# An LSTM with a three-layer sign-weight network: where x's later quarters are split into high and low parts

## What is computed

```python
def lstm_forward(x, h0, Wx, Wh, b):          # x (32, 64, 256), Wx and Wh (256, 1024)
    xW = einsum('ntd,dg->ntg', x, Wx) + b
    def step(carry, xw_t):
        prev_h, prev_c = carry
        a = xw_t + prev_h @ Wh
        i, f, o = sigmoid(a[:, :256]), sigmoid(a[:, 256:512]), sigmoid(a[:, 512:768])
        g = tanh(a[:, 768:])
        next_c = f * prev_c + i * g
        next_h = o * tanh(next_c)
        return (next_h, next_c), next_h
    ...                                       # 64 steps, one after the other

def ffn(x, k0, k1, k2, s0, s1, s2):           # boolean k: weights are +1 or -1
    h = concatenate([x, -x], axis=-1)
    h = relu(s0 * dense(k0, h)) * 2           # 512 -> 1024
    h = relu(s1 * dense(k1, h)) * 2           # 1024 -> 1024
    return s2 * dense(k2, h)                  # 1024 -> 256

return x + ffn(lstm_forward(x, cond_1024, Wx, Wh, b), ...)
```

## Time and profile before

| what | value |
|---|---|
| three runs | 293.06, 294.0, 294.33 us, median 294.0 |
| the profiled execution | 293.16 us, of which the span 291.4 |
| mean granted clock of TensorE | 0.988 of full speed |
| busy: TensorE matmuls | 277.7 us, 95% of the span |
| busy: VectorE, ScalarE, GpSimd | 206.2, 153.1, 12.0 us |

### The profile page before, as it was taken

One profiled execution on the slowest core, in us unless ns is written; L12 is line 12 of the kernel. 1 busy time (PEld: TensorE's weight loads), 2 busy tenths in 40 slices (PEclk: granted clock), 3 DMA queues, 4 the chain that ended last, 5 costly groups with the idle time before them and its releaser, 6 DMA issues.

```text
span 291.4 us, 8783 instructions
## 1 busy us (share of the span) xinstructions
PE 277.7 (95%) x3608; PEld 224.1 (77%) x3608; DVE 206.2 (71%) x749; ACT 153.1 (53%) x470; POOL 12.0 (4%) x19
## 2 busy tenths in 40 slices
PE   7947997999999999999999999999999999999995
PEld 5835876776799898999989999999999996544441
DVE  2842888877878888888888888888888876531013
ACT  4662564576666655655656556565566544411110
POOL 0108031000000000000000000000000000000000
PEclk9995999999999999999999999999999999999999
DMA  7950000000000000100000001000100100010001
GB/s 191 403 240 2 1 3 2 0 2 2 1 2 2 2 4 2 38 2 3 9 31 3 2 3 38 2 2 3 38 1 2 38 3 2 0 36 2 0 0 72
DMA packets 4791, 8.72 MB, mean 30 GB/s; under 512 B 912, under 2 KB 2448, under 8 KB 4624
## 3 DMA queue, kind: packets, MB, share of 16 engines
q1 hardware_dynamic: 4176, 7.87, 7.6%
q10 hardware_dynamic: 576, 0.30, 0.3%
HBM read 6.07 MB, written 2.10 MB: 28 GB/s over the span
## 4 chain that ended last, share of the span: by engine, by line
PE 74%; DVE 10%; ACT 5%; issue 4%; DMA 3%; SPq 2%; POOL 1%; POOLq 0%; DVEq 0%
PE WK L390 45%; PE ACC L403 9%; PE G L355 9%; PE G L346 8%; PE WK L373 4%; DMA x<-in_x 3%; ACT tT L530 3%; DVE aT L679 2%; DVE cD L690 1%; DVE uT L688 1%; ACT tC L535 1%; DVE xw L586 1%; DVE h L571 1%; POOL xs L727 1%; DVE h L696 1%
## 5 line engine op out<-in xcount | busy, mean ns | idle before, releaser
L390 PE MATMUL WK<-h,k 128*128 128x256 f16 (+1 forms) x992 | 126.9, 276 | 0.1
L390 PEld LDWEIGHTS WK<-h,k 128*128 128x128 fp8e5 x992 | 93.6, 98 | 16.0 <-issue 1.9
L530 ACT ACTIVATE tT<-aT 128x128 f32<-128x128 f32 x126 | 39.0, 310 | 64.2 <-DVE aT L679 62.9
L571 DVE SCALAR_TENSOR_TENSOR h<-WK,h 128x256 f16<-128x256 f32 (+1 forms) x104 | 42.3, 437 | 27.2 <-ACT h L493 27.2
L679 DVE TENSOR_REDUCE aT<-G 128x128 f32<-128x256 f32 x128 | 48.2, 417 | 15.5 <-PE G L355 14.8
L493 ACT ACTIVATE h<-WK 128x256 f16<-128x256 f32 (+1 forms) x104 | 37.2, 388 | 30.0 <-PE WK L390 29.8
L373 PE MATMUL WK<-xs,wxs 128*128 128x512 f32 x168 | 45.7, 412 | 6.2 <-POOL xs L727 5.7
L475 ACT ACTIVATE G<-xw 128x256 f32<-128x256 f32 x126 | 46.6, 370 | 0.0
L373 PEld LDWEIGHTS WK<-xs,wxs 128*128 128x128 f32 x168 | 30.7, 193 | 13.0 <-POOL xs L727 7.0
L346 PEld LDWEIGHTS G<-h,w 128*128 128x128 f16 x1008 | 32.7, 96 | 8.9 <-DVE h L696 6.2
L355 PE MATMUL G<-h,w 128*128 128x64 f16 x1008 | 39.5, 192 | 0.0
(11 more groups left out here) (63 smaller groups left out, 142.2 us busy)
## 6 DMA issues: line engine op xcount, KB each, us to landing
x<-in_x SPq DMA_DIRECT2D x3, 512.0 KB, 8.9
out_y<-x SPq DMA_DIRECT2D x12, 128.0 KB, 1.8
xw<-in_wx SPq DMA_DIRECT2D x4, 256.0 KB, 6.2
xw<-in_wh SPq DMA_DIRECT2D x4, 256.0 KB, 6.5
k<-in_k SPq DMA_DIRECT2D x1, 1024.0 KB, 11.0
k<-in_k SPq DMA_DIRECT2D x1, 512.0 KB, 8.2
out_y<-x SPq DMA_DIRECT2D x2, 256.0 KB, 2.0
x<-in_x ACTq DMA_DIRECT2D x1, 256.0 KB, 4.3
```

Of the source, the lines that this page charges most:

```text
L390: ins = eng.matmul(layer_src(tile), w, rhs, start=a == 0, stop=last)
L530: eng.activation(tT[:, B * j0:B * j1], aT[:, j0:j1].rearrange("p j b -> p (j b)"), ACT.Tanh, scale=half_gain0 if t == 0 else half_gain).th ...
L571: eng.scalar_tensor_tensor(layer_dst(tile, 1), layer_src(tile), 0.0, layer_dst(tile, 0), ALU.max, ALU.subtract).then_inc(lo_made[tile[0]])
```

## The change

1. GpSimd keeps only the two casts of quarter 1 (semaphore `xh1`). Its six subtractions and the other four casts go.
2. The low parts of quarter 1 are made by VectorE ahead of step 0, between `w_lo` and the low part of h0. Quarters 2 and 3 are split by ScalarE (`x_hi`) and VectorE (`x_lo`), one half after each of the steps 2, 3 (quarter 2) and 4, 5 (quarter 3). On ScalarE the split stands ahead of the step's tiles.
3. Tiles of quarters 1 to 3 are all emptied by ScalarE; VectorE empties only tile (0, 4). The six matmuls of such a tile now use the low part of x last.
4. `w0_make` comes after the steps 1, 6, 7; `w2_make` after 6; `w1_make` is two operations on 1024 words, after 8 and 9, of the kind with one tensor input and two operands of one value for each partition (`seven`, `sign1`).
5. Ahead of step 0, `w_max(3)` comes ahead of `wx_lo(2)`, and `wx_lo(3)` comes behind the scales; on ScalarE tile (0, 3) is emptied between the halves of `w_hi`.
6. The order of quarter 3's tiles and of the first layer's first chunk is shifted by a place.

```diff
-X_DVE = ((4,), (2, 5), (2, 5), (2, 5))
+X_DVE = ((4,), (), (), ())
-W0_STEPS = (1, 3, 4)
-W1_STEPS = (5, 6, 7, 9)
-W2_STEPS = (11,)
+X2_STEPS = (2, 3)
+X3_STEPS = (4, 5)
+W0_STEPS = (1, 6, 7)
+W1_STEPS = (8, 9)
+W2_STEPS = (6,)
...
-        order += [((0, 0, m), 4), (("x", 3, m), 6)]
+        order += [(("x", 3, n), 6) for n in range(NJ) if (0, 1, 2, 4, 5, 6, 7, 8)[n] == m] + [((0, 0, m), 4)]
+    order.append((("x", 3, 7), 6))
...
+                if i:
+                    k, wp, xp = ((0, 0, 0), (0, 1, 0), (1, 0, 0), (1, 1, 0), (0, 0, 1), (1, 0, 1))[a]
...
-            def x_hi(k):
-                e.wait_ge(dx0[k], 16)
-                eng.activation(xs[:, 0, 0, k, :], x[:, 0, k], ACT.Copy).then_inc(xh)
+            def x_hi(i, k):
+                if i == 0:
+                    e.wait_ge(dx0[k], 16)
+                else:
+                    e.wait_ge(dx[i - 1], 16)
+                    e.wait_ge(x_mm, NJ * (i - 1))
+                eng.activation(xs[:, i % 2, 0, k, :], x[:, i, k], ACT.Copy).then_inc(xh)
...
+                if t in X2_STEPS:
+                    x_hi(2, X2_STEPS.index(t))
+                if t in X3_STEPS:
+                    x_hi(3, X3_STEPS.index(t))
                 for tile in act_plan[t]:
...
             def w1_make(n):
-                part = k1[:, 512 * n:512 * n + 512]
+                part = k1[:, 1024 * n:1024 * n + 1024]
                 e.wait_ge(dk1, 16)
-                eng.scalar_tensor_tensor(part, part, 7, sign1[:, :].broadcast_to((P, 512)), ALU.logical_shift_left,
-                                         ALU.bitwise_xor).then_inc(w1_made)
+                eng.tensor_scalar(part, part, seven[:, :], sign1[:, :], ALU.logical_shift_left,
+                                  ALU.bitwise_xor).then_inc(w1_made)
...
             w_max(2)
-            wx_lo(2)
             w_max(3)
...
-            wx_lo(3)
+            wx_lo(2)
             e.wait_ge(max_all, 1)
...
+            wx_lo(3)
             x_empty(("x", 0, 4))
             for g in range(4):
                 w_lo(g)
+            x_lo(1, 0)
+            x_lo(1, 1)
...
-            for i in range(1, NQ):
...
-                for k in range(2):
...
-                    eng.tensor_tensor(lo, x[:, i, k], hi.bitcast(F32), ALU.subtract).then_inc(xp_lo)
+            eng.wait_ge(dx[0], 16)
+            for k in range(2):
+                eng.tensor_copy(xs[:, 1, 0, k, :], x[:, 1, k]).then_inc(xh1)
```

More of the change, by code:

```diff
@@ L118, in ready @@
         if tile[0] == "x":
-            inputs = t >= (-1, -1, 2, 6)[tile[1]]
+            inputs = t >= (-1, -1, 4, 6)[tile[1]]
         elif tile[0] == 0:
@@ L211, in lstm_ffn @@
         sign1 = sb("sign1", [P, 1], U32)
+        seven = sb("seven", [P, 1], U32)
         h1 = sb("h1", [P, 8192], F16)
@@ L366, in x_matmul @@
                     e.wait_ge(wxh, j // 2 + 1)
[L367 to L370, removed]
+                if xp:
+                    e.wait_ge(xl, 2 * i + k + 1)
+                elif i == 1:
+                    e.wait_ge(xh1, k + 1)
                 else:
-                    e.wait_ge(xp_lo if xp else xp_hi, 2 * (i - 1) + k + 1)
+                    e.wait_ge(xh, 2 * max(i - 1, 0) + k + 1)
                 ins = eng.matmul(TILE[bank[tile]][:, :], wxs[:, wp, j, k], xs[:, i % 2, xp, k], start=a == 0, stop=a == 5)
@@ L386, in layer_matmul @@
                     e.wait_ge(lo_made[0], 8 * c + k + 1)
-                    e.wait_ge(w1_made, 4)
+                    e.wait_ge(w1_made, 2)
                     w, rhs = w1[:, k, 128 * m:128 * m + 128], h1s[c][:, k, part]
@@ L472, in seed @@
                     wait_x_out(e, ("x", t // 16, 3 if t == 0 and g == 0 else 7))
-                    wait_x_out(e, ("x", t // 16, X_DVE[t // 16][-1]))
+                    if t == 0 and g == 1:
+                        wait_x_out(e, ("x", 0, 4))
                 src = xw[:, t // 4, 4 * g:4 * g + 4].rearrange("p j (t b) -> p j t b", t=4)[:, :, t % 4]
@@ L501, in _ @@
             wx_hi(0)
-            x_hi(0)
-            x_hi(1)
+            x_hi(0, 0)
+            x_hi(0, 1)
             wx_hi(1)
@@ L509, in _ @@
             wx_hi(3)
+            w_hi(0)
+            w_hi(1)
             x_empty(("x", 0, 3))
-            for g in range(4):
-                w_hi(g)
+            w_hi(2)
+            w_hi(3)
             e.wait_ge(scaled, 4)
@@ L563, in w_lo, with x_lo @@
                 eng.scalar_tensor_tensor(lo, src, scale2 if g == 0 else scale, hi, ALU.mult, ALU.subtract).then_inc(wlo)
-            def x_lo(k):
-                e.wait_ge(xh, k + 1)
-                eng.tensor_tensor(xs[:, 0, 1, k, :], x[:, 0, k], xs[:, 0, 0, k, :].bitcast(F32), ALU.subtract).then_inc(xl)
+            def x_lo(i, k):
+                if i == 1:
+                    e.wait_ge(xh1, k + 1)
+                else:
+                    e.wait_ge(xh, 2 * max(i - 1, 0) + k + 1)
+                eng.tensor_tensor(xs[:, i % 2, 1, k, :], x[:, i, k], xs[:, i % 2, 0, k, :].bitcast(F32),
+                                  ALU.subtract).then_inc(xl)
             def layer_lo(tile):
@@ L613, in signs @@
                 e.wait_ge(signed, 6)
+                e.wait_ge(zeroed, 3)
             def w0_make(n):
@@ L621, in w0_make @@
                 elif n == 1:
-                    eng.scalar_tensor_tensor(b, b, 7, sign0[:, :].broadcast_to((P, 512)), ALU.logical_shift_left,
-                                             ALU.bitwise_xor).then_inc(w0_made)
+                    eng.tensor_scalar(b, b, seven[:, :], sign0[:, :], ALU.logical_shift_left,
+                                      ALU.bitwise_xor).then_inc(w0_made)
                 else:
@@ L639, in _ @@
             wx_lo(0)
-            x_lo(0)
-            x_lo(1)
+            x_lo(0, 0)
+            x_lo(0, 1)
             e.wait_ge(db, 16)
@@ L701, in _ @@
                     signs()
+                if t in X2_STEPS:
+                    x_lo(2, X2_STEPS.index(t))
+                if t in X3_STEPS:
+                    x_lo(3, X3_STEPS.index(t))
                 if t in W0_STEPS:
@@ L716, in _ @@
             eng.memset(mx[:, 4:5], 2.0 ** -67).then_inc(zeroed)
+            eng.memset(seven[:, :], 7).then_inc(zeroed)
             eng.wait_ge(maxed, 7)
             eng.partition_all_reduce(max2[:, :], mx[:, 6:8], P, bass.bass_isa.ReduceOp.max).then_inc(max_all)
-            for i in range(1, NQ):
-                eng.wait_ge(dx[i - 1], 16)
-                if i >= 2:
-                    eng.wait_ge(x_mm, NJ * (i - 1))
-                for k in range(2):
-                    hi, lo = (xs[:, i % 2, part, k, :] for part in range(2))
-                    eng.tensor_copy(hi, x[:, i, k]).then_inc(xp_hi)
-                    eng.wait_ge(xp_hi, 2 * (i - 1) + k + 1)
-                    eng.tensor_tensor(lo, x[:, i, k], hi.bitcast(F32), ALU.subtract).then_inc(xp_lo)
+            eng.wait_ge(dx[0], 16)
+            for k in range(2):
+                eng.tensor_copy(xs[:, 1, 0, k, :], x[:, 1, k]).then_inc(xh1)
 def kernel(x, cond_1024, L0_cond_Wx, L0_cond_Wh, L0_cond_b, L0_ffn_k0, L0_ffn_k1, L0_ffn_k2, L0_ffn_s0, L0_ffn_s1,
```

2 lines of the change are left out of this document (1 added, 1 removed).

## The result

| | before | changed |
|---|---|---|
| median | 294.13 us (4 runs, 293.06 to 294.33) | 282.56 us (4 runs, 282.07 to 283.00) |
| profiled execution, span | 293.16, 291.4 | 282.9, 281.1 |

The ratio is 0.961 (95% interval 0.958 to 0.964). The forecast was 283.6 and the range 282.0 to 286.5. Against the profiled execution the sum gave 282.8, and that execution took 282.9.

A forecast was written before the change was run, and what follows sets the result against it. Bound by TensorE's own work from about 30 us on, at the start by GpSimd's wait. 6.2 us (start) plus 4.4 (steps) less 0.2 (small waits) is 10.4; 294.0 − 10.4 = 283.6 us, range 282.0 to 286.5.

The forecast's parts named there:

- the 8.08 us: Ahead of step 0: GpSimd's unexplained wait between its first cast and first subtraction, read as a code change, expected to go.
- (a): Step 0 takes 4.24 us where 3.50 would do; all of the excess was to go.
- (b): One VectorE operation in step 0 takes 1.25 us, one in step 4 1.31, against a 242 ns mean; to go.
- (c): Several steps late because VectorE has two pieces, 1.26 us together, before the next reduce: 3.59 us where 3.26 would do.
- The stop has a second price: Ahead of step 0, TensorE's clock falls to 0.50 after its stop: four x matmuls take 2.71 us, ten 2.54 at full speed.
- The pairing at no cost: Splitting x behind steps 2 to 5 costs nothing while TensorE's filler covers it; narrowest margin 0.1 to 0.2 us, at step 6.
- The weights: Four 683 ns operations become two on twice the words: about 0.7 us each at the low end (taken), 1.2 high.
- 1: Rival: pairing not covered in steps 2 to 5, costing 0.3 to 1.17 us each; 284.8 to 288.3 us; chance 0.20.
- 2: Rival: GpSimd's wait stays, ahead of its second cast; step 0 begins at about 25.8; about 290 us; chance 0.06.
- 3: Rival: GpSimd's second cast blocks VectorE through the port, start 0.6 us later; 284.2 us; chance inside the forecast's 0.70.
- 4: Rival: ScalarE waits for x's third quarter ahead of step 3's tanh; 296 us if it lands at 42; chance 0.02.
- my case: Span of the forecast: 282.0 us (start at 19.5, no small waits, against profiled execution) to 285.0 (port, slow `w1_make`).

The follow-up runs named there:

- the last three runs: Changed kernel with VectorE's old order ahead of step 0, 283.14 us; with high-part products first, 282.80; with that and two more matmuls ahead of step 0, 283.94.

## Why the prediction was right

**The start, 6.2 us forecast, 6.18 measured.** TensorE's chain was forecast to begin step 0 at 20.0 and it was 20.01. VectorE was forecast to be done at 19.4 and was at 19.81; 0.3 of the difference is `wx_lo(3)` held by the second cast. ScalarE was forecast at 19.6 to 19.8 and its last seed ended at 19.93. That the start came out to 0.01 is luck: four runs with the same order ahead of step 0 began it at 19.97, 20.23, 20.43 and 20.73, as the inputs landed sooner or later. The reading of the 8.08 us as a change of GpSimd's code after the maximum fits four runs: gone without the maximum (two runs), back with one subtraction behind it, and moved with the first subtraction. What is loaded there the profile doesn't show. As for the Trainium skill's "GPSIMD Engine Reference", section 2.1: the waits were 6.76 to 8.57 us here and not about 6, and the two runs without the maximum show none.

**The steps, 4.2 us forecast (4.4 less 0.2), 4.26 measured.** The floor of 43.6 us from counts and rates was 43.78. Of the split, (a) is right in size, 0.76 us, and 0.66 of it was the clock. The first half of (b), the operation held in step 0, cost little: with the clock kept up another one is held there (the high part of h, 1.00 us for 0.23), and the step takes 3.58, 0.10 more than in the changed kernel. (b) holds for step 4, 1.66 us (4.94 to 3.28): that step is as short with only the later quarters moved (3.27) and as long as before with only quarter 1 moved (4.95). (c) is 0.31 at step 2, 0.26 at step 7, 0.35 at step 11 and 0.52 at step 12 (4.26 to 3.74), each with the same matmuls before and after. "The stop has a second price" was too much for the four matmuls ahead of step 0: all but some 0.26 us of theirs was covered.

**The pairing at no cost** held, with the margin of 0.1 to 0.2 us: steps 3 to 6 take 3.50, 3.28, 3.50 and 3.28, TensorE's own time, and the run with a doubled rounding shows that there was hardly more. One term of the working does not come out of its numbers: 2.11 and three pieces of 0.57 are 3.82, not 3.88. In the trace the tanh of step 3 begins 3.84 us behind step 2's first reduce (31.45 against 27.61).

**The weights.** Low end 0.7, high end 1.2; these rows by form measured:

```profile
L653 DVE TENSOR_SCALAR k<-k,seven,sign 128x1024 uint32<-128x1024 uint32 x2 | 1.6, 808 | 0.0
...
L644 DVE TENSOR_SCALAR k<-k,seven,sign 128x512 uint32<-128x512 uint32 x1 | 0.5, 541 | 0.0
L658 DVE TENSOR_SCALAR k<-k 128x512 uint32<-128x512 uint32 x1 | 0.4, 420 | 0.0
```

It is the fast kind. L644 and L658 do the same two operations on 512 words and differ only in their two operands, from memory or in the instruction: 0.12 us, from one pair of rows. The estimate of 0.70 from the Trainium skill's page "VectorE: DVE Perf Modes", section "Side-by-side: where the cycles go", is low by 0.11.

**The rivals.** 1 did not happen, but the margin was as thin as I said. 2 did not: the second cast follows the first. 3 happened in half: 0.3 us on VectorE, none on step 0. 4 did not. The ends of my case are a little wide: by the terms named they are 282.1 and 284.7, not 282.0 and 285.0. The forecast of 283.6 was 1.0 above the median, and 0.84 of it is the median of before over its profiled execution, which I added; the changed kernel's median is 0.3 below its own. So the sum was right for the pair of traces, 10.4 against 10.3, while the medians lie 11.6 apart.

## What to carry to other kernels

A wait on GpSimd that the profile lays to nothing, behind an operation of another family, is worth moving away from, and removing the wait alone is not enough: GpSimd's operations then fall beside VectorE's and hold them, and TensorE's stops behind those can bring its clock down as well. Where every step is bound by TensorE's filler, count the matmuls of a stretch times their start-to-start time: that floor was right to 0.2 us in 44 here and gives what all the stalls together can be worth. A kernel whose chains have been made level gains nothing from mending one of them, as the last three runs show. And when an edit feeds a planner, count each step's work again before reading its length as a wait.

## What was not expected

The set-up row for the subtraction's code stands in the order without the maximum too, and costs nothing there; I had taken the row for the wait. TensorE's slow clock cost some 0.9 us by the trace, 1.4 by the executions that kept it, and not the 1.5 to 2.2 I had expected, because the wait beside it covered much of the rest. And one GpSimd subtraction of 1.26 us holds a VectorE operation on a single element for each partition until it ends, 1.09 us in place of 0.15.
